# A mixed attention and expert layer on one core: the shared network's odd 64 inner rows stacked, 17 down products a token tile in place of 18

## What is computed

```python
def _swiglu_mlp(x, wg, wu, wd):
    return jax.nn.silu(x @ wg) * (x @ wu) @ wd
...
return y + _swiglu_mlp(identity, sw_gate, sw_up, sw_down)
```

## Time and profile before

| What | Value |
|---|---|
| runs of the kernel | 1048.69, 1052.60, 1054.52 us (median 1052.6) |
| the profiled execution, its own time | 1049.94 us |
| its span from first to last instruction | 1048.2 us |
| mean granted clock of TensorE, share of full speed | 0.938 |
| busy: PE / VectorE / ScalarE / GpSimd | 948.5 / 652.3 / 541.1 / 319.2 us |

### The profile page before, as it was taken

How to read it: one execution, slowest core, us unless ns; L and a number is a source line. 1 busy time by engine, 2 the same in 40 slices (tenths; PEclk the granted TensorE clock), 3 DMA queues, 4 the chain that set the end, 5 groups by cost and what they waited for, 6 DMA issues and landing times.

```text
span 1048.2 us, 17957 instructions
## 1 busy us (share of the span) xinstructions
PE 948.5 (90%) x5671; PEld 637.8 (61%) x5672; DVE 652.3 (62%) x1082; ACT 541.1 (52%) x821; POOL 319.2 (30%) x303
## 2 busy tenths in 40 slices
PE   2694699999999995989999999999999999999997
PEld 2592599999999992344545545545545545545445
DVE  6669863334333445667677686677676676776652
ACT  2322444444444442556566566566566566565562
POOL 1000222222222201424334244244145145145142
PEclk9755599999999995799999999999999999999999
DMA  8587425422222214644655645646645555543210
GB/s 261 201 321 247 137 75 157 134 68 71 69 70 70 77 49 121 189 114 107 184 145 132 190 132 137 188 128 146 186 129 140 182 138 145 164 109 91 53 58 21
DMA packets 93936, 139.85 MB, mean 133 GB/s; under 512 B 18120, under 2 KB 51344, under 8 KB 92848
## 3 DMA queue, kind: packets, MB, share of 16 engines
q1 hardware_dynamic: 87392, 121.32, 40.2%
q0 software_dynamic: 6480, 17.70, 5.8%
HBM read 79.57 MB, written 54.71 MB: 128 GB/s over the span
## 4 chain that ended last, share of the span: by engine, by line
PE 71%; DVE 13%; ACT 7%; issue 5%; DMA 3%; SPq 1%; DVEq 0%; ACTq 0%
PE bank L1232 10%; PE st_pair L1243 8%; PE bank L1294 8%; PE bank L1138 7%; PE s_pair L1120 7%; PE bank L1255 7%; PE st_pair L1120 6%; PE s_pair L1194 5%; ACT prob L933 5%; DVE top L1622 4%; PE bank L1128 2%; DVE h_f L1646 2%; PE bank L1027 2%; PE bank L1103 2%; PE bank L1265 1%
## 5 line engine op out<-in xcount | busy, mean ns | idle before, releaser
L1622 DVE TENSOR_REDUCE top<-s_pair 128x2 f32<-128x1024 f32 x252 | 308.7, 1225 | 153.6 <-PE s_pair L1194 152.1
L933 ACT ACTIVATE prob<-st_pair 128x1024 f32<-128x1024 f32 x256 | 260.7, 1018 | 174.5 <-PE st_pair L1243 169.7
L737 POOL TENSOR_TENSOR h_T<-h_f,h_T 128x512 fp32r<-128x512 f32 (+1 forms) x48 | 61.5, 1282 | 351.9 <-ACT h_T L915 351.9
L715 POOL DMA_INDIRECT xg<-xn_rows,token_of x71 | 68.9, 971 | 298.8 <-PE bank L1103 182.2
L1243 PEld LDWEIGHTS st_pair<-q_rows,k_rows 50*128 50x128 f32 x512 | 48.6, 186 | 165.7 <-ACT prob L933 125.2
L1232 PE MATMUL bank<-xT_b,w_sh 128*128 128x512 f32 x528 | 144.9, 410 | 0.0
L1243 PE MATMUL st_pair<-q_rows,k_rows 50*128 50x512 f32 x512 | 130.2, 504 | 15.6 <-ACT prob L933 10.3
L1255 PE MATMUL bank<-prob,v_ones 128*32 128x512 f32 x1024 | 138.8, 615 | 0.0
L1194 PE MATMUL s_pair<-k_rows,q_rows 48*128 48x512 f32 x504 | 113.2, 441 | 5.9 <-DVE top L1622 5.1
L1232 PEld LDWEIGHTS bank<-xT_b,w_sh 128*128 128x128 f32 x528 | 93.4, 189 | 31.0 <-issue 11.8
L1138 PE MATMUL bank<-w_exp,c_hT 128*128 (+1 forms) x639 | 93.6, 291 | 1.0 <-ACT c_y L868 1.0
(11 more groups left out here) (214 smaller groups left out, 1172.9 us busy)
## 6 DMA issues: line engine op xcount, KB each, us to landing
qk_rows<-qk_hi SPq DMA_DIRECT2D x56, 256.0 KB
q_rows<-qk_rows SPq DMA_DIRECT2D x64, 192.0 KB
k_rows<-qk_rows SPq DMA_DIRECT2D x56, 192.0 KB
expert_rows<-c_y SPq DMA_DIRECT2D x71, 128.0 KB, 1.7
xn_T_split<-x_T SPq DMA_DIRECT2D x8, 1024.0 KB, 4.6
xT_b<-xn_T_split SPq DMA_DIRECT2D x32, 256.0 KB, 4.6
qk_rows<-qk_lo SPq DMA_DIRECT2D x28, 256.0 KB
x_all<-in_L_attn_x_dram SPq DMA_DIRECT2D x8, 512.0 KB, 5.6
```

Of the source, the lines that this page charges most:

```text
L715: pool.indirect_dma_start(xg[s % 4][:, :], None, xn_dram, bass.IndirectOffsetOnAxis(token_of[:, s:s + 1], 0)).then_inc(c_x[s % 4], 16)
L737: pool.tensor_tensor(h_T[0:m, LO, f, :], h_f[q % 2][0:m, :], h_T[0:m, HI, f, :].bitcast(F32), ALU.subtract).then_inc(p_h, 1)
L933: act.activation(prob[kt % 2][:, 2 * jp:2 * jp + 2, :].rearrange("p j l -> p (j l)"), st_pair[:, :], ACT.Exp, scale=HD ** -0.5).then_inc(a ...
L1622: dve.tensor_reduce(top[g % 2][:, :, jp, qt], score_pair(b, g, v)[:, :].rearrange("p (i k) -> p i k", i=2), AX_X, ALU.max).then_inc(d_max, 1)
```

## The change

The low part of the odd group is written by VectorE, not by GpSimd, and it goes to partitions 64 to 127 of `h_T[:, HI, 5]`, right under the high part in 0 to 63. The odd 64 rows of the down weights are loaded twice, to partitions 0 to 63 and to 64 to 127 (a seventh load). So one product with 128 rows gives high x high + low x high, and one with 64 rows gives high x low: 17 products a tile. VectorE's new instruction has its place at step (1, 7), behind that step's maximum. GpSimd's `hidden_low(b, 1)` is gone, so `p_h` counts five a batch (`lows`), and a new semaphore `d_hl` stands for the odd group in `tanh(b, 3)` and in the first down tile.

```diff
+        STACK = 64 + SF_LAST
+        def lows(b, q):
+            return b * (SFT - 1) + ups(q) + 1
...
                 else:
-                    to, of_w = dn[0:SF_LAST, SFT - 1, :], sw_down[(SFT - 1) * P:SF, :]
+                    o = 64 * (n - 5)
+                    to, of_w = dn[o:o + SF_LAST, SFT - 1, :], sw_down[(SFT - 1) * P:SF, :]
...
-                if 8 <= s < 14:
+                if 8 <= s < 15:
                     load_shared(s - 8)
...
                 hidden_low(b, 0)
                 if there(b - 1):
                     ao_low(b - 1, 1)
-                hidden_low(b, 1)
                 for n in range(4):
                     scale_y(b, n)
...
             def tanh(b, q):
                 wait(act, b_g, b * SFT + q + 1)
-                wait(act, p_h, b * SFT + q - 1)
+                if q == BOTH + 2:
+                    wait(act, d_hl, b + 1)
+                elif q >= 2:
+                    wait(act, p_h, lows(b, q - 2))
+                elif b:
+                    wait(act, p_h, lows(b - 1, q + SFT - 2))
...
-            act.wait_ge(s_in, 96)
+            act.wait_ge(s_in, 112)
...
+            DOWNS = []
+            for q in range(SFT):
+                DOWNS += [(q, P, a, c) for a, c in PRODUCTS] if q != BOTH else [(q, STACK, HI, HI), (q, SF_LAST, HI, LO)]
...
-                for i in range(18):
-                    q, (a, c) = i // 3, PRODUCTS[i % 3]
-                    m, f = rows_of(q), ORDER[q]
-                    if t == 0 and i % 3 == 0:
-                        wait(pe, p_h, b * SFT + q + 1)
+                for i, (q, m, a, c) in enumerate(DOWNS):
+                    f = ORDER[q]
+                    if t == 0 and (i == 0 or q != DOWNS[i - 1][0]):
+                        wait(pe, p_h, lows(b, q)) if q != BOTH else wait(pe, d_hl, b + 1)
...
+            def hidden_low_both(b):
+                wait(dve, a_hh, b * SFT + BOTH + 1)
+                dve.tensor_tensor(h_T[64:STACK, HI, SFT - 1, :], h_f[BOTH][0:SF_LAST, :], h_T[0:SF_LAST, HI, SFT - 1, :].bitcast(F32),
+                                  ALU.subtract).then_inc(d_hl, 1)
...
                     if what == "out":
                         low_rank_o_low(c)
+                    if (g, t) == (1, 7) and there(b):
+                        hidden_low_both(b)
```

More of the change, by code:

```diff
@@ L334, in build_program @@
         b_to, b_bo, d_iv, d_to, a_bo, d_bo = (sem(n) for n in ("b_to", "b_bo", "d_iv", "d_to", "a_bo", "d_bo"))
+        d_hl = sem("d_hl")
         p_h = sem("p_h")
@@ L1288, in down_shared @@
                     wait(pe, d_dn, b * TPB + t - 1)
-                for i in range(18):
-                    q, (a, c) = i // 3, PRODUCTS[i % 3]
-                    m, f = rows_of(q), ORDER[q]
-                    if t == 0 and i % 3 == 0:
-                        wait(pe, p_h, b * SFT + q + 1)
+                for i, (q, m, a, c) in enumerate(DOWNS):
+                    f = ORDER[q]
+                    if t == 0 and (i == 0 or q != DOWNS[i - 1][0]):
+                        wait(pe, p_h, lows(b, q)) if q != BOTH else wait(pe, d_hl, b + 1)
                     ins = pe.matmul((g_bank, u_bank)[t % 2][:, 0:D], h_T[0:m, a, f, t * P:(t + 1) * P],
-                                    w_sh[0:m, c, S_GU + f * D:S_GU + (f + 1) * D], start=(i == 0), stop=(i == 17))
+                                    w_sh[0:m, c, S_GU + f * D:S_GU + (f + 1) * D], start=(i == 0), stop=(i == len(DOWNS) - 1))
                 ins.then_inc(b_dn, 1)
```

## The result

The changed kernel takes **1048.51 us** (median of 22 runs, 1043.97 to 1051.05); in the same comparison the kernel before takes 1051.97 us. The ratio is 0.9965 with a 95% interval of 0.9952 to 0.9979: 3.7 us of 1052 less (2.2 to 5.0), where 3.45 were forecast.

What follows compares the result with a forecast made beforehand. TensorE's products in the 32 down tiles were taken to set the end: -3.8 us for one product less a tile, +0.35 for VectorE's new instruction, so 1052.6 - 3.45 = 1049.1 us (0.33% less), range 1045.4 to 1053.0.

Steps and rivals of the forecast that it cites:

- TensorE's down tiles are the path: All 32 down tiles: time their products lose on TensorE is won by the kernel, the last four tiles included.
- Rival 2: Down step ended by another engine, or first tiles wait for GpSimd: nothing won, 1052.6 us, chance 0.1; in part 1050.0.
- A product is worth 0.118 us, not the mean of 0.152: Down tile: the removed 64-row product saves one ordinary interval of 0.118 us, not 2.73 us averaged over 18 products.
- a term of 3.8: Down tiles on TensorE: one product less in each, 32 x 0.118 = 3.8 us won, bounds nothing to 4.9.
- Rival 4: Down tile's products rearrange since loads set the pace: 4.9 us won by the mean price, 1047.7 us, chance 0.05.
- Both changes of shape stay: Down tile: switches between 128-row and 64-row products remain, two gaps of 0.32 us, together 0.20 us each above ordinary steps.
- rival 1: Down tile: a lone 64-row product makes the change of shape cheaper; 9.9 us won, 1042.7 us, chance 0.1.
- VectorE's new instruction, 0.35 us: Step (1, 7): a weighing beside it makes the next maximum 0.05 us late in seven batches, 0.35 us lost, bounds 0 to 1.3.
- the carried-over wait: Step (1, 7): VectorE's new instruction ends 0.55 us behind GpSimd's last weighing, at 612.63, as in the earlier trace.
- The contended row: Earlier trace: line 1668 on VectorE took 1.36 us, twice its time, with GpSimd busy beside it from 1014.90 to 1017.27.
- What else moves is hidden: Other edits cost nothing: GpSimd's relief, first tile's low part (margin 0.31 to 0.19 us), new semaphore, seventh weight load.
- Rival 3: VectorE's queue at step (1, 7): new instruction delays the maximum of (2, 0) by 1.5 us; 8 us slower, 1061, chance 0.05.

Runs made afterwards that it cites:

- e1_all128: Against the changed kernel, the lone 64-row product of the odd group reads 128 rows, adding low x low: 1091.26 us, ratio 0.9831 to the kernel before.
- e5_pool_keeps: Against the changed kernel, GpSimd also keeps its own subtraction for the odd group, beside VectorE's: 1102.89 us, ratio 0.9926 to the kernel before.
- e4_move_only: Against the changed kernel, 18 products again, VectorE still computes the low part but writes it to the old place: 1109.34 us, ratio 1.0003 to the kernel before.
- e6_three_dve: Against the changed kernel, VectorE's new instruction runs three times, the added two written where nothing reads: 1110.51 us, ratio 1.0001 to the kernel before.

## Why the prediction was right

1. **TensorE's down tiles are the path.** Right. Seven batches lost 3.40 us for 28 tiles, the end of the kernel too: VectorE waits 3.38 us for the last tile in place of 3.50. Rival 2 falls.
2. **A product is worth 0.118 us, not the mean of 0.152.** Right: 2.73 to 2.61 us a tile, and 3.9 us from the first down tile to the end against a term of 3.8. The removed product had neighbours of its own shape. Rival 4 falls.
3. **Both changes of shape stay.** Right: gaps of 0.32 and 0.31 us around the lone product, and rival 1 falls. Its price of 0.20 us each was right too (0.19 by e1_all128). The reserve that this left in the kernel, 10 us and more, was in the earlier trace rows, and the prediction didn't follow it up, since the change leaves it there.
4. **VectorE's new instruction, 0.35 us.** This term was wrong: it measured nothing, within the bounds of 0 to 1.3. Its time was read right, 0.69 us against 0.68 from the earlier trace rows, and so was its place beside the fourth weighing. What failed is the carried-over wait. The prediction let VectorE end 0.55 us behind GpSimd, as in the earlier trace rows; it ended 0.09 us behind it (613.61 against 613.52), after 0.74 us, and 0.46 us were left to the next maximum. The contended row had a TENSOR_TENSOR of GpSimd beside it that took 2.37 us; the weighing is a TENSOR_SCALAR with one tensor operand that takes 0.91. The rule of the Trainium skill, SBUF — State Buffer, section "Who interferes with whom", takes in every GpSimd instruction that reads SBUF. The runs agree with that for both kinds: VectorE waited for GpSimd's TENSOR_TENSOR (1440 ns), and the weighing of e5_pool_keeps waited for VectorE (1.45 us in place of 0.91). What doesn't fit is the hold for the whole instruction that the prediction took from it: the weighing of the changed kernel had started 0.26 us before VectorE's instruction and had 0.65 us to go, but held it back by 0.05. How long within its 0.91 us a weighing stands in the way was not measured. The next step of the term fits: where the maximum was 0.24 us late (e5_pool_keeps), 0.26 us a batch were lost.
5. **What else moves is hidden.** Right for VectorE (e4_move_only, within 0.3%) and for the first tile of a batch, whose last three products didn't wait in the changed kernel. It was nearer than it looked: with 0.37 us less in front of them they wait 0.19 us. The new semaphore is set at 613.61, 13 us before `tanh(b, 3)` (626.92), not some 9; that changes nothing.
6. **Rival 3, a loss by VectorE's queue.** It didn't come, and e6_three_dve shows that its mechanism was real: 1.46 us more on that queue cost about 7 us.

The forecast of 1049.1 us stands 0.6 us above the measured 1048.5, and this 0.6 us is the difference between the two medians of the kernel before (1052.6 and 1051.97). That the gain then meets the forecast's to a tenth is in part luck: its interval is 1.4 us to either side, so this time tells neither 3.45 from 3.8 nor either from the 4.9 of the mean price. The rows of the tiles do. The lower edge of the range, 1045.4, lies 2.3 us under 1047.7, not the 2 that the text names; nothing hangs on it.

## What to carry to other kernels

Read a row of products as single loads before you price one: here the mean of 0.152 us was made of 0.118 us steps and two changes of shape at 0.19 us, and the odd shape was worth three times the product that the change removed. Padding an odd product to the full 128 rows, with operands that are there anyway, is then the larger gain than saving one; when the tile gets shorter, look which operand is late next and put its product last. A time under contention is carried over only for the same pair of instructions in the same order: here one order cost VectorE 0.05 us, and the other cost GpSimd 0.54.

## What the runs showed of the hardware that was not expected

- A VectorE TENSOR_TENSOR with two SBUF inputs (64x512) takes 0.69 us alone and 0.74 when GpSimd's TENSOR_SCALAR on an SBUF tile (128x256) has started 0.26 us before it. Where VectorE's instruction has the way first, that TENSOR_SCALAR takes 1.45 us in place of 0.91. Beside GpSimd's TENSOR_TENSOR, VectorE's stands until that ends, 1.44 us in all.
- A lone fp32r product with 64 rows between products with 128 costs TensorE 0.50 us, of which 0.13 are the product.
- On three other chips the kernel before takes 1110 to 1112 us in place of 1052, and the changed one 1101 (on one of them) in place of 1048.5. Behind the second down tile of each batch TensorE's signals come late (5.2 to 5.9 us behind the last down load's end in the changed kernel again, where it was 0.22) and four of them within 0.18 us, VectorE and ScalarE stand for 5 to 8 us, and TensorE comes back at 1.2 GHz for 6.8 to 10.2 us. The cause is open.
